# Attention on one core: one exponential less on ScalarE in every third unit, and a rounding copy on VectorE

## Chip, cores and metric

The kernel runs on one core of one Trainium2 chip (trn2). The metric is the device time of one execution in microseconds. Engines are named as in the profile: PE is TensorE's matmul, PEld its weight load, DVE is VectorE, ACT is ScalarE, POOL is GpSimd, SP is the engine that issues most DMAs.

## What is computed

A transformer block in fp32 on 48 x 48 tokens of 384 channels: layer norm, attention with 12 heads and a relative position bias, then a mixture-of-experts feed-forward. The change touches attention alone:

```python
attn = jnp.einsum('bqd,bkd->bqk', q * scale, k)
bias = (rel_h[..., :, None] + rel_w[..., None, :]).reshape(B * nh, S, S)
attn = jax.nn.softmax(attn + bias, axis=-1)
out = jnp.einsum('bqk,bkd->bqd', attn, v)
```

## The kernel before

TensorE multiplies in fp32r, a 4-byte type of less precision, so a value that needs full precision is kept as a pair: a high part, rounded to fp32r, and a low part, the value less its high part. Both go through TensorE.

A head has 2304 queries and 2304 keys. The queries are cut into 3 blocks of 768 columns (QBLOCKS = 3, QB = 768), the keys into 18 tiles of 128 rows (TILES = 18). One key tile against one query block is a **unit**: 54 units a head (UNITS), 648 in 12 heads. A unit goes through these steps:

- `scores`, TensorE, L851 to L865: four matmuls of 384 columns make the scores, 128 keys by 768 queries, in two of the four banks of ps_s. The bias and the subtraction of the row's maximum are in the operands (query_rest has the maximum in its last row).
- `exps`, ScalarE, L924 to L936: an exponential of the scores goes to p_hi, rounded to fp32r (L930), and a second exponential of the same scores goes to p_f in fp32 (L936). p_hi has a ring of 4 buffers, p_f has 2, so the second exponential of a unit waits until the low part two units back is made (L935).
- `low`, L718 to L723: p_lo = p_f - p_hi. VectorE makes it for two units of three and GpSimd (POOL) for the third, the one whose index leaves 2 when divided by POOL_EVERY = 3. `lo_done` (L712) gives the semaphore and the count for each.
- `pv`, TensorE, L867 to L875: four matmuls of the value tile with p_hi and p_lo add up the outputs and the softmax sums in ps_o, over the 18 units of a block.

The row maxima of the next head are made beside that. In each unit TensorE computes a chunk of 128 queries by 768 keys from the high parts alone, in two halves (`half`, L845), each into its own bank of ps_m, and VectorE reduces each half to a maximum (`reduce_half`, L971). A half is not started before the last one in its bank is reduced (L901, L910). When a query block is complete, a small maximum over the chunks gives neg_m (L969), which TensorE transposes, ScalarE copies, and SP takes to memory and back into query_rest.

The order is written out by hand for each engine, and each engine works through its own list in order. In step k of a head TensorE issues: the scores of unit k + 3 (LEAD), the first half of the chunk, pv of unit k, the second half (L877 to L911). VectorE issues: the maximum of the first half, the low part of unit k + 2 (LOW_LEAD) unless GpSimd has it, the maximum of the second half (L976 to L994). In the last unit of each block ScalarE and VectorE each copy half of ps_o to o_t (L945, L983). GpSimd's list (L827 to L841) is its low parts in order; behind two of the six of each block it also joins two partial outputs of a finished block: a copy of 32x384 (L821) and a sum of 32x384 (L823). In the last head the maxima end with step 11 (SHIFT = 12), since there is no next head: 606 units have maxima, 42 have none.

What the change touches: the semaphore at L687, which L930 signals and nothing waits for; `low` for GpSimd's units at L827 to L839; `exps` at L930; and VectorE's list at L989 to L991.

Of the kernel before, what the change touches and what calls it, by code (L numbers as in the profile page):

```python
# [12 lines left out]
ACT = mybir.ActivationFunctionType  # L13
# [11 lines left out]
TB = 384  # L25
# [353 lines left out]
UNITS = QBLOCKS * TILES  # L379
# [3 lines left out]
LOW_LEAD = 2  # L383
POOL_EVERY = 3
SHIFT = 12
RING = 4
# [257 lines left out]
def phase_attention(nc, q_hi_d, q_lo_d, k_hi_d, k_lo_d, rel_hi_d, rel_lo_d, v_d, m_d, o_d, sums_d, ident, keys, query_hi0, query_rest0, val0, mx, room):  # L644
# [11 lines left out]
    with ExitStack() as ctx:  # L656
        def sb(name, shape, dt=F32):
            return ctx.enter_context(nc.sbuf_tensor(name, shape, dt))

        def sem(name):  # L660
            return ctx.enter_context(nc.semaphore(name))
# [6 lines left out]
        p_hi = [sb(f"p_hi{i}", [P, 2, TB], F32R) for i in range(RING)]  # L668
        p_lo = [sb(f"p_lo{i}", [P, 2, TB], F32R) for i in range(RING)]
        p_both = sb("p_f", [P, 2, 2, TB])  # L670
        p_f = [p_both[:, i, :, :] for i in range(2)]
# [6 lines left out]
        ps_s = ctx.enter_context(nc.psum_tensor("ps_s", [P, 4, 512], F32))  # L678
# [5 lines left out]
        rest_in = [sem(f"rest_in{i}") for i in range(QBLOCKS)]  # L684
        m_out = sem("m_out")
        s_ok = sem("s_ok")
        hi_ok = sem("p_hi_ok")  # L687
        f_ok = sem("f_ok")
        lo_dve = sem("p_lo_dve")
        lo_pool = sem("p_lo_pool")  # L690
# [17 lines left out]
        def unit_at(par, k, lead=LEAD):  # L708

            return (par, k + lead) if k + lead < UNITS else (1 - par, k + lead - UNITS)  # L710

        def lo_done(h, idx):  # L712

            if idx % POOL_EVERY == POOL_EVERY - 1:
                return lo_pool, UNITS // POOL_EVERY * h + idx // POOL_EVERY + 1
            return lo_dve, (UNITS - UNITS // POOL_EVERY) * h + idx - idx // POOL_EVERY + 1

        def low(engine, n, par, idx):  # L718

            r = (2 * par + idx) % RING  # L720
            engine.wait_ge(f_ok, n + 3)
            engine.tensor_tensor(p_lo[r][:], p_f[idx % 2], p_hi[r][:].bitcast(F32),  # L722
                                 ALU.subtract).then_inc(lo_done(0, idx)[0], 1)  # L723
# [81 lines left out]
        @block.gpsimd  # L805
        def _(pool):
            for g in range(2):
                pool.sem_inc(ot_out[g], 32)
            def joined(h, par, b, c):

                g = (QBLOCKS * par + b) % 2

                pool.wait_ge(acc_a if c == 0 else acc_d, QBLOCKS * h + b + 2)
                at = TILES * (b + 1) + (1 + c) * POOL_EVERY - 1
                if at < UNITS:
                    pool.wait_ge(*lo_done(h, at))
                elif h < HEADS - 1:
                    pool.wait_ge(*lo_done(h + 1, at - UNITS))
                elif c == 0:
                    pool.wait_ge(*lo_done(h, UNITS - 1))  # L820
                pool.tensor_copy(o_low[g][:, c, :], o_t[g][HD:2 * HD, c, :]).then_inc(low_moved, 1)  # L821
                pool.wait_ge(low_moved, 2 * (QBLOCKS * h + b) + c + 1)
                pool.tensor_tensor(o_s[g][:, c, :], o_t[g][0:HD, c, :], o_low[g][:, c, :], ALU.add).then_inc(o_sum, 1)  # L823

            FIRST = 3 * POOL_EVERY

            def head(h, par, last=False):  # L827
                for idx in range(FIRST - 1, UNITS + FIRST - 1, POOL_EVERY):
                    if idx < UNITS:
                        low(pool, UNITS * h + idx, par, idx)  # L830
                    elif not last:
                        low(pool, UNITS * h + idx, 1 - par, idx - UNITS)
                    for b in range(QBLOCKS):
                        for c in range(2):
                            if idx == TILES * (b + 1) + (1 + c) * POOL_EVERY - 1:
                                joined(h, par, b, c)

            for idx in range(POOL_EVERY - 1, FIRST - 1, POOL_EVERY):
                low(pool, idx, 0, idx)  # L839
            for h in range(HEADS):  # L840
                head(h, h % 2, h == HEADS - 1)  # L841
# [80 lines left out]
        @block.scalar  # L922
        def _(act):
            def exps(h, par, idx, turn=None):  # L924
                n = UNITS * h + idx
                bank, r = 2 * (idx % 2), (2 * par + idx) % RING
                act.wait_ge(s_ok, n + 1)

                act.wait_ge(pv_ok, n + 1)
                act.activation(p_hi[r][:], ps_s[:, bank:bank + 2, 0:TB], ACT.Exp).then_inc(hi_ok, 1)  # L930
                if turn is not None:
                    act.copy(neg_mt[turn][:], ps_s[0:6, bank, TB:TB + P]).then_inc(negt_ok, 1)

                if UNITS * h + idx >= 2:
                    act.wait_ge(*(lo_done(h, idx - 2) if idx >= 2 else lo_done(h - 1, idx - 2 + UNITS)))  # L935
                act.activation(p_f[idx % 2], ps_s[:, bank:bank + 2, 0:TB], ACT.Exp).then_inc(f_ok, 1)  # L936

            def head(h, par, last=False):
                for k in range(UNITS):
                    if k % TILES == TILES - 1:  # L940
                        b = k // TILES
                        g = (QBLOCKS * par + b) % 2
                        act.wait_ge(pv_ok, UNITS * h + k + 1 + RING)
                        act.wait_ge(ot_out[g], out_count(h, par, b))
                        act.copy(o_t[g][:, 0, :], ps_o[0:VW, 0, 0:TB]).then_inc(acc_a, 1)  # L945
                    up, idx = unit_at(par, k)
                    if not (last and up != par):
                        exps(h + (up != par), up, idx, turned_at(k, last))

            def out_count(h, par, b):  # L950
                return 32 * ((QBLOCKS * par + b) // 2) + 32 * QBLOCKS * half(h, par) + 32

            def half(h, par):
                return (h - par) // 2

            act.sem_inc(acc_a, 1)
            act.sem_inc(f_ok, 2)
            for idx in range(LEAD):
                exps(0, 0, idx)
            for h in range(HEADS):  # L960
                head(h, h % 2, h == HEADS - 1)

        @block.vector
        def _(dve):
            def negated(count, s):

                if s % TILES == TILES - 1:
                    dve.wait_ge(mx_ok, 2 * count + 2)
                    dve.tensor_reduce(neg_m[s // TILES][:], mx[s // TILES][:], AX.X, ALU.max, negate=True).then_inc(neg_ok, 1)  # L969

            def reduce_half(count, s, c):  # L971
                dve.wait_ge(mm_ok, 2 * count + c + 1)
                col = s % 3 * 2 + c
                dve.tensor_reduce(mx[s // TILES][:, s // 3 % 6, col:col + 1], ps_m[:, c, 0:TB], AX.X, ALU.max).then_inc(mx_ok, 1)  # L974

            def head(h, par, last=False):  # L976
                for k in range(UNITS):
                    if k % TILES == TILES - 1:
                        b = k // TILES
                        g = (QBLOCKS * par + b) % 2  # L980
                        dve.wait_ge(pv_ok, UNITS * h + k + 1 + RING)
                        dve.wait_ge(ot_out[g], out_count(h, par, b))
                        dve.tensor_copy(o_t[g][:, 1, :], ps_o[0:VW, 1, 0:TB]).then_inc(acc_d, 1)  # L983
                    tp, s = chunk_at(h, par, k)
                    maxima = not (last and tp != par)
                    number = UNITS * (h + 1) + k - SHIFT
                    if maxima:
                        reduce_half(number, s, 0)
                    up, idx = unit_at(par, k, LOW_LEAD)  # L989
                    if not (last and up != par) and idx % POOL_EVERY < POOL_EVERY - 1:  # L990
                        low(dve, UNITS * h + k + LOW_LEAD, up, idx)  # L991
                    if maxima:
                        reduce_half(number, s, 1)
                        negated(number, s)  # L994

            def out_count(h, par, b):
                return 32 * ((QBLOCKS * par + b) // 2) + 32 * QBLOCKS * half(h, par) + 32

            def half(h, par):
                return (h - par) // 2  # L1000

            dve.sem_inc(acc_d, 1)
            dve.sem_inc(pv_ok, RING)
            dve.sem_inc(mm_ok, 2 * (UNITS - SHIFT))
            dve.sem_inc(mx_ok, 2 * (UNITS - SHIFT))
            dve.sem_inc(neg_ok, 2)
            for idx in range(LOW_LEAD):
                if idx % POOL_EVERY < POOL_EVERY - 1:
                    low(dve, idx, 0, idx)
            for h in range(HEADS):  # L1010
                head(h, h % 2, h == HEADS - 1)
# [889 lines left out]
```

## Time and profile before

| | us |
|---|---|
| median of 3 runs | 2230.9 |
| lowest and highest | 2229.8, 2233.19 |
| the profiled execution | 2227.99 |
| its span | 2226.2 |
| TensorE busy, share of the span | 94% |
| VectorE | 80% |
| ScalarE | 74% |
| GpSimd | 34% |

The span runs from the first to the last instruction in the trace; the time of the execution has a little around it. Attention lies between about 270 and 1418 us of the span. A duration in the views is that of the instruction from start to end; consecutive instructions of one engine overlap a little, so what one occupies is read from start to start.

### The profile page before, as it was taken

To read this page: it belongs to the slowest core of one execution; us is meant where nothing else is said; L and a number is where in the kernel's file an instruction comes from. 1 tells how busy PE (TensorE), PEld (TensorE's weight loads), DVE (VectorE), ACT (ScalarE), POOL (GpSimd) and SP (SyncE) were. 2 spreads that over 40 slices of the span, in tenths; PEclk is the share of its full clock that TensorE was granted. 3 is DMA by queue.
4 is the path that set the end of the run, shared out by engine and by line. 5 is a ranking of instruction groups with operands and counts; after the bars stand their busy time and mean duration, and the time that the engine had idled before them with its cause. 6 is when DMAs were issued, how large, how long until landed. Compare 5 with 4: busy or idle time off the path is not lost. (4 is left out here: it accounts for less than half of the span.)

```text
span 2226.2 us, 38086 instructions
## 1 busy us (share of the span) xinstructions
PE 2092.3 (94%) x12644; PEld 1936.4 (87%) x12644; DVE 1773.6 (80%) x3334; ACT 1650.6 (74%) x2908; POOL 755.4 (34%) x519
## 2 busy tenths in 40 slices
PE   6977899999999999999999999675999999999997
PEld 6977788888888888888888888463999999999997
DVE  5667899998999999999999996476777777777774
ACT  3354488888888888888888889412787777778785
POOL 0060045544444454454445545511121221111211
PEclk9955599999999999999999999786999999999999
DMA  6889876554655556365545632323666767666774
GB/s 212 240 246 301 249 136 107 106 102 74 133 88 109 90 106 117 74 117 102 107 83 101 131 75 70 98 106 108 198 219 216 222 220 221 216 217 215 215 219 108
DMA packets 121594, 338.20 MB, mean 152 GB/s; under 512 B 17984, under 2 KB 57496, under 8 KB 114740
## 3 DMA queue, kind: packets, MB, share of 16 engines
q1 hardware_dynamic: 109152, 308.88, 53.9%
q0 software_dynamic: 10400, 19.87, 4.1%
q10 hardware_dynamic: 1920, 7.88, 1.3%
q8 instruction: 69, 1.13, 0.2%
q14 instruction: 53, 0.43, 0.1%
HBM read 269.62 MB, written 66.97 MB: 151 GB/s over the span
## 5 line engine op out<-in xcount | busy, mean ns | idle before, releaser
L974 DVE TENSOR_REDUCE mx<-ps_m 128x1 f32<-128x384 f32 x1212 | 642.1, 552 | 100.8 <-PE ps_m L849 95.4
L722 POOL TENSOR_TENSOR p_lo<-p_f,p_hi 128x768 fp32r<-128x768 f32 x216 | 401.1, 1857 | 680.7 <-ACT p_f L936 680.7
L930 ACT ACTIVATE p_hi<-ps_s 128x768 fp32r<-128x768 f32 x648 | 528.4, 815 | 139.2 <-PE ps_s L863 135.9
L936 ACT ACTIVATE p_f<-ps_s 128x768 f32<-128x768 f32 x648 | 525.1, 810 | 1.3 <-POOL p_lo L722 1.3
L722 DVE TENSOR_TENSOR p_lo<-p_f,p_hi 128x768 fp32r<-128x768 f32 x432 | 418.9, 970 | 31.7 <-ACT p_f L936 30.8
L849 PE MATMUL ps_m<-all_keys,query_hi 128*128 128x384 f32 x1212 | 409.1, 342 | 7.6 <-DVE mx L974 7.6
L1644 ACT CAST w_hi<-w_raw 128x384 fp32r<-128x384 f32 x600 | 290.3, 516 | 134.2 <-PE ps_o L1621 128.3
L1762 DVE TENSOR_TENSOR w_lo<-w_raw,w_hi 128x384 fp32r<-128x384 f32 x600 | 316.5, 555 | 76.9 <-ACT w_hi L1644 76.7
L860 PE MATMUL ps_s<-query_hi,all_keys 128*128 128x384 f32 x1296 | 336.0, 340 | 5.0 <-SPq L783 4.1
L873 PE MATMUL ps_o<-p_hi,val 128*65 128x384 f32 x1296 | 330.8, 336 | 1.9 <-POOL p_lo L722 1.7
L863 PE MATMUL ps_s<-query_rest,all_keys 121*128 121x384 f32 x1296 | 331.8, 337 | 0.0
L873 PE MATMUL ps_o<-p_lo,val 128*65 128x384 f32 x1296 | 331.7, 337 | 0.0
L849 PEld LDWEIGHTS ps_m<-all_keys,query_hi 128*128 128x128 f32 x1212 | 226.9, 188 | 45.4 <-DVE mx L974 21.4
L1580 POOL DMA_INDIRECT out<-y,to_i x50 | 80.2, 1604 | 522.6 <-ACT y L1676 361.3
L860 PEld LDWEIGHTS ps_s<-query_hi,all_keys 128*128 128x128 f32 x1296 | 231.7, 188 | 15.2 <-SPq L782 4.5
L863 PEld LDWEIGHTS ps_s<-query_rest,all_keys 121*128 121x128 f32 x1296 | 236.9, 189 | 0.0
L873 PEld LDWEIGHTS ps_o<-p_lo,val 128*65 128x65 f32 x1296 | 175.3, 135 | 50.2
L1621 PE MATMUL ps_o<-w_hi,h_hi 128*128 128x384 f32 x600 | 206.7, 344 | 0.0
L1621 PE MATMUL ps_o<-w_hi,h_lo 128*128 128x384 f32 x600 | 202.8, 338 | 0.0
L1621 PE MATMUL ps_o<-w_lo,h_hi 128*128 128x384 f32 x600 | 202.6, 338 | 0.0
L873 PEld LDWEIGHTS ps_o<-p_hi,val 128*65 128x65 f32 x1296 | 176.0, 136 | 29.4 <-POOL p_lo L722 4.2
L1798 DVE TENSOR_TENSOR h_lo<-h_f,h_hi 128x256 fp32r<-128x256 f32 x300 | 127.6, 425 | 42.8 <-ACT h_f L1670 37.5
(199 smaller groups left out, 2999.0 us busy)
## 6 DMA issues: line engine op xcount, KB each, us to landing
w_raw<-w_u SPq DMA_DIRECT2D x200, 576.0 KB, 4.8
query_rest<-rel_lo_d SPq DMA_DIRECT2D x36, 864.0 KB
query_rest<-q_hi_d SPq DMA_DIRECT2D x36, 576.0 KB
query_rest<-q_lo_d SPq DMA_DIRECT2D x36, 576.0 KB
rel_hi_d<-room SPq DMA_DIRECT2D x6, 2016.0 KB, 13.7
rel_lo_d<-out_lo SPq DMA_DIRECT2D x6, 2016.0 KB, 18.6
query_hi<-rel_hi_d SPq DMA_DIRECT2D x24, 432.0 KB, 18.8
v_d<-v_sb SPq DMA_DIRECT2D x6, 1170.0 KB, 8.0
```

The costliest lines, as they stand in the source:

```text
L722: engine.tensor_tensor(p_lo[r][:], p_f[idx % 2], p_hi[r][:].bitcast(F32), ALU.subtract).then_inc(lo_done(0, idx)[0], 1)
L849: pe.matmul(ps[:, c, 0:TB], query_hi[tp][:, tile], key_hi[tp][:, keys], start=True, stop=True).then_inc(mm_ok, 1)
L860: pe.matmul(ps_s[:, bank + c, 0:TB], key_hi[par][:, j * P:(j + 1) * P], query_hi[par][:, b * QB + c * TB:b * QB + (c + 1) * TB], start=Tru ...
L863: last = pe.matmul(ps_s[:, bank + c, 0:TB], key_rest[par][:, j * P:(j + 1) * P], query_rest[b][0:TOP, j // 3, c * TB:(c + 1) * TB], start= ...
L873: last = pe.matmul(ps_o[0:VW, c, 0:TB], val[par][:, j, :], part[r][:, c, :], start=(j == 0 and part is p_hi), stop=(j == TILES - 1 and par ...
L930: act.activation(p_hi[r][:], ps_s[:, bank:bank + 2, 0:TB], ACT.Exp).then_inc(hi_ok, 1)
L936: act.activation(p_f[idx % 2], ps_s[:, bank:bank + 2, 0:TB], ACT.Exp).then_inc(f_ok, 1)
L974: dve.tensor_reduce(mx[s // TILES][:, s // 3 % 6, col:col + 1], ps_m[:, c, 0:TB], AX.X, ALU.max).then_inc(mx_ok, 1)
L1621: mm = pe.matmul(ps_o[:, t, 0:C], v[w][:, f, cut], wt[w][:, f, :], start=(q + f + m == 0), stop=(q == QUARTERS - 1 and f == FC - 1 and m = ...
L1644: act.copy(hi[par][:, j % KC, :], raw[par][:, j % KC, :]).then_inc(whi_ok, 1)
L1762: low = dve.tensor_tensor(lo[par][:, k, :], raw[par][:, k, :], hi[par][:, k, :].bitcast(F32), ALU.subtract)
L1798: dve.tensor_tensor(h_lo[w][:, f, :], h_f[:, f, :], h_hi[w][:, f, :].bitcast(F32), ALU.subtract).then_inc(g_lo, 1)
```

## The change

In GpSimd's units ScalarE leaves out the exponential into p_hi. VectorE fills p_hi by a copy of p_f that rounds to fp32r, at the place in its list where it makes the low part of other units. GpSimd waits for that copy (semaphore cast_ok) before its low part. The old semaphore p_hi_ok goes. 648 exponentials into p_hi become 432; 216 copies of 128x768 are new; all else stands as it was.

```diff
--- before.py
+++ after.py
@@ -684,7 +684,7 @@
         rest_in = [sem(f"rest_in{i}") for i in range(QBLOCKS)]
         m_out = sem("m_out")
         s_ok = sem("s_ok")
-        hi_ok = sem("p_hi_ok")
+        cast_ok = sem("cast_ok")
         f_ok = sem("f_ok")
         lo_dve = sem("p_lo_dve")
         lo_pool = sem("p_lo_pool")
@@ -715,6 +715,9 @@
                 return lo_pool, UNITS // POOL_EVERY * h + idx // POOL_EVERY + 1
             return lo_dve, (UNITS - UNITS // POOL_EVERY) * h + idx - idx // POOL_EVERY + 1
 
+        def rounded_by_dve(idx):
+            return idx % POOL_EVERY == POOL_EVERY - 1
+
         def low(engine, n, par, idx):
 
             r = (2 * par + idx) % RING
@@ -826,6 +829,8 @@
 
             def head(h, par, last=False):
                 for idx in range(FIRST - 1, UNITS + FIRST - 1, POOL_EVERY):
+                    if idx < UNITS or not last:
+                        pool.wait_ge(cast_ok, (UNITS * h + idx) // POOL_EVERY + 1)
                     if idx < UNITS:
                         low(pool, UNITS * h + idx, par, idx)
                     elif not last:
@@ -836,6 +841,7 @@
                                 joined(h, par, b, c)
 
             for idx in range(POOL_EVERY - 1, FIRST - 1, POOL_EVERY):
+                pool.wait_ge(cast_ok, idx // POOL_EVERY + 1)
                 low(pool, idx, 0, idx)
             for h in range(HEADS):
                 head(h, h % 2, h == HEADS - 1)
@@ -927,7 +933,8 @@
                 act.wait_ge(s_ok, n + 1)
 
                 act.wait_ge(pv_ok, n + 1)
-                act.activation(p_hi[r][:], ps_s[:, bank:bank + 2, 0:TB], ACT.Exp).then_inc(hi_ok, 1)
+                if not rounded_by_dve(idx):
+                    act.activation(p_hi[r][:], ps_s[:, bank:bank + 2, 0:TB], ACT.Exp)
                 if turn is not None:
                     act.copy(neg_mt[turn][:], ps_s[0:6, bank, TB:TB + P]).then_inc(negt_ok, 1)
 
@@ -987,7 +994,10 @@
                     if maxima:
                         reduce_half(number, s, 0)
                     up, idx = unit_at(par, k, LOW_LEAD)
-                    if not (last and up != par) and idx % POOL_EVERY < POOL_EVERY - 1:
+                    if not (last and up != par) and rounded_by_dve(idx):
+                        dve.wait_ge(f_ok, UNITS * h + k + LOW_LEAD + 3)
+                        dve.tensor_copy(p_hi[(2 * up + idx) % RING][:], p_f[idx % 2]).then_inc(cast_ok, 1)
+                    elif not (last and up != par):
                         low(dve, UNITS * h + k + LOW_LEAD, up, idx)
                     if maxima:
                         reduce_half(number, s, 1)
```

## Rows read from the trace of the kernel before

**Rows 1.** Busy time by stretch: us, busy (count) per engine, PEclk, DMA share, GB/s.
```profile
700.00:800.00 100.00, 99.42 (x566) 89.19 (x565) 90.30 (x157) 86.61 (x119) 48.08 (x31) 1.00 0.56 102
```

**Rows 2.** Costliest groups, whole span: busy us, mean ns, idle before and its releaser.
```profile
L974 DVE TENSOR_REDUCE mx<-ps_m 128x1 f32<-128x384 f32 x1212 | 642.1, 552 | 100.8 <-PE ps_m L849 95.4
...
L930 ACT ACTIVATE p_hi<-ps_s 128x768 fp32r<-128x768 f32 x648 | 528.4, 815 | 139.2 <-PE ps_s L863 135.9
```

**Rows 3.** VectorE in time, one cycle: start us, us, what, [idle before <-releaser].
```profile
827.88 1.01 DVE L974 TENSOR_REDUCE mx<-ps_m 128x1 f32<-128x384 f32 x2
829.11 0.56 DVE L974 TENSOR_REDUCE mx<-ps_m 128x1 f32<-128x384 f32 x1 [0.23 <-PE ps_m L849]
829.99 0.56 DVE L974 TENSOR_REDUCE mx<-ps_m 128x1 f32<-128x384 f32 x1 [0.32 <-PE ps_m L849]
830.46 0.95 DVE L722 TENSOR_TENSOR p_lo<-p_f,p_hi 128x768 fp32r<-128x768 f32 x1
831.33 1.02 DVE L974 TENSOR_REDUCE mx<-ps_m 128x1 f32<-128x384 f32 x2
832.26 0.95 DVE L722 TENSOR_TENSOR p_lo<-p_f,p_hi 128x768 fp32r<-128x768 f32 x1
833.13 1.01 DVE L974 TENSOR_REDUCE mx<-ps_m 128x1 f32<-128x384 f32 x2
```

**Rows 4.** GpSimd in time, the same cycle.
```profile
827.91 1.85 POOL L722 TENSOR_TENSOR p_lo<-p_f,p_hi 128x768 fp32r<-128x768 f32 x1 [0.88 <-ACT p_f L936]
833.13 1.85 POOL L722 TENSOR_TENSOR p_lo<-p_f,p_hi 128x768 fp32r<-128x768 f32 x1 [3.38 <-ACT p_f L936]
```

**Rows 5.** All engines in time, 1338.9 to 1341.3 us.
```profile
1338.92 1.01 POOL L823 TENSOR_TENSOR o_s<-o_t,o_low 32x384 f32<-32x384 f32 x1
...
1338.94 1.81 DVE L722 TENSOR_TENSOR p_lo<-p_f,p_hi 128x768 fp32r<-128x768 f32 x1
...
1340.67 1.01 DVE L974 TENSOR_REDUCE mx<-ps_m 128x1 f32<-128x384 f32 x2
...
1341.27 0.19 PEld L849 LDWEIGHTS ps_m<-all_keys,query_hi 128*128 128x128 f32 x1 [0.78 <-DVE mx L974]
```

**Rows 6.** GpSimd and VectorE in time, where the maxima have ended.
```profile
1357.63 1.84 POOL L722 TENSOR_TENSOR p_lo<-p_f,p_hi 128x768 fp32r<-128x768 f32 x1 [2.96 <-ACT p_f L936]
...
1358.97 1.32 DVE L722 TENSOR_TENSOR p_lo<-p_f,p_hi 128x768 fp32r<-128x768 f32 x1 [2.07 <-ACT p_f L936]
...
1364.76 1.04 POOL L821 COPY o_low<-o_t 32x384 f32<-32x384 f32 x1
```

**Rows 7.** A wider maximum (groups), and one-input operations on SBUF (VectorE in time).
```profile
L598 DVE TENSOR_REDUCE mx<-ps_c 128x2 f32<-128x768 f32 x42 | 39.4, 949 | 14.2 <-PE ps_c L528 13.8
...
1524.01 0.29 DVE L1708 TENSOR_SCALAR sel<-rank 128x144 fp32r<-128x144 f32 x1 [2.52 <-POOL every L1556]
...
1524.44 0.23 DVE L1710 TENSOR_SCALAR first<-rank 128x144 f32<-128x144 f32 x1
...
1531.04 0.17 DVE L1739 TENSOR_SCALAR row_i<-at_i 128x36 int32<-128x36 int32 x1
```

**Rows 8.** TensorE in time, the same cycle.
```profile
830.48 0.34 PE L849 MATMUL ps_m<-all_keys,query_hi 128*128 128x384 f32 x1
...
831.52 0.51 PE L873 MATMUL ps_o<-p_hi,val 128*65 128x384 f32 x2
...
832.22 0.34 PE L849 MATMUL ps_m<-all_keys,query_hi 128*128 128x384 f32 x1
```

**Rows 9.** VectorE: first and last maximum, a neg_m maximum, and the copy's group.
```profile
271.99 0.56 DVE L974 TENSOR_REDUCE mx<-ps_m 128x1 f32<-128x384 f32 x1 [0.25 <-PE ps_m L849]
...
1352.80 0.55 DVE L974 TENSOR_REDUCE mx<-ps_m 128x1 f32<-128x384 f32 x1
...
1353.39 0.19 DVE L969 TENSOR_REDUCE neg_m<-mx 128x6 f32<-128x36 f32 x1
...
L983 DVE COPY o_t<-ps_o 65x384 f32<-65x384 f32 x36 | 19.6, 545 | 3.7 <-PE ps_o L873 3.7
```

## The prediction, made before the changed kernel was seen

> **What bounds the kernel now.** I read the stretch view first. In 700 to 800 us, the middle of attention, TensorE is busy 99.42 of 100 us at the full granted clock, VectorE 90.30, ScalarE 86.61, GpSimd 48.08 [rows 1]. So TensorE sets the pace and VectorE stands close behind it; an exponential taken from ScalarE lightens an engine that is third. The groups give the counts: 1212 half-block maxima, two for each of 606 units, and 648 exponentials of 0.815 us into p_hi [rows 2].
>
> Then one cycle of three units in order of time. I call A a unit whose low part GpSimd makes, and A+1 and A+2 the two behind it, whose low parts VectorE makes. VectorE's list [rows 3]: two maxima back to back take 1.01 us against 0.55 for one, so one occupies it for 0.46; from the start of such a pair to the next instruction it is 0.93 (831.33 to 832.26); a low part occupies 0.87 (830.46 to 831.33). The only idle time is 0.23 + 0.32 = 0.55 us, ahead of two maxima and ended by TensorE. The cycle lasts 5.22 to 5.25 us (827.88 to 833.13); GpSimd's low parts start 5.22 us apart [rows 4], and I take 5.23. GpSimd's low part of A takes 1.85 us, 827.91 to 829.76; VectorE's low part of A+1 starts 0.70 us later, at 830.46. The two never overlap, and that is an accident of when each gets its input.
>
> What happens if they do overlap is in two other places. At 1338.92 GpSimd starts a 1.01 us sum; VectorE's low part, sent 0.02 us later, lasts 1.81 us in place of 0.95, and the next maximum starts at 1340.67, 0.74 us after GpSimd's end at 1339.93. TensorE then waits 0.78 us for that maximum [rows 5]. And at 1358.97 a low part comes in the middle of GpSimd's of 1357.63 to 1359.47 and ends at 1360.29, 0.82 us after GpSimd's end [rows 6]. So a low part on VectorE does not run beside GpSimd's: it waits for nearly all of the rest of it, and TensorE has no store of work to cover that.
>
> **The change, part by part.**
>
> Removed: 216 exponentials of 0.815 us on ScalarE [rows 2]. Worth nothing in time: ScalarE's own idle time, 139.2 us, ends by TensorE's scores in 135.9 of it [rows 2], and TensorE is busy beside it. The input p_f of A is there up to 0.8 us earlier, but the new reader is VectorE, whose list is in order, and the cast stands behind the first maximum of step A-2. The 216 skipped signals of the old semaphore had no reader.
>
> Added on VectorE: 216 casts of 128x768 from p_f to p_hi, SBUF to SBUF. The trace has none. Upper end: one element at a time, as the low part: 0.95 long, 0.87 occupied [rows 3]; a 128x768 maximum says the same, 0.949 [rows 7]. Lower end: the one-input operations on SBUF. With 36 columns one takes 0.17, with 144 columns 0.23 [rows 7], so 108 more cost about 0.06, or 0.55 ns a column; the maxima pay 949 - 552 = 397 ns for 384 more, or 1.03 [rows 2, 7]. At 0.55 a cast of 768 is 0.17 + 732 x 0.55 ns = 0.57. I take 0.55 long and 0.46 occupied, as a 384-column maximum. Against it speaks the one such row that writes the cast's type, fp32r: 0.29 for 144 columns; but it also reads its input reordered, so I give the slow cast a lesser chance. By the Trainium skill, VectorE: DVE Perf Modes, the perf-mode tier table, an fp32 tensor_copy between SBUF tensors goes two elements a cycle; worked out from its 1227 ns for 2048 elements and 0.96 GHz that is an estimate of 0.56 us here, and the sum would stay as below.
>
> Moved: GpSimd's low part of A starts after the cast instead of after the exponential. In the cycle shown, the first maximum of step A-2 starts at 827.88 + 0.46 = 828.34, the cast at 828.80, so GpSimd starts at 828.80 + 0.55 + 0.08 (its start behind the exponential, as now within 0.1 us) = 829.43 and ends at 831.28, not 829.76. That covers the moment at which VectorE wants its low part of A+1, 830.46. This is the step that costs. Behind the blocked low part on VectorE's queue stand the maxima, which TensorE waits for, since its two banks of ps_m are refilled only when read.
>
> The new cycle, counted from the start of the cast, VectorE's list: cast 0 to 0.46; two maxima, 0.46 to 1.39; low part of A+1 asks at 1.39. GpSimd runs from 0.55 + 0.08 = 0.63 to 2.48. The low part then lets the next start 0.74 after that [rows 5], 3.22. Two maxima to 4.15; low part of A+2 to 5.02; two maxima to 5.95; next cast. Is VectorE ever idle in it? TensorE issues its half of step A once the maximum at 3.22 is done (3.77); its weights come in 0.05 later and take 0.19 [rows 5], the matmul 0.34 [rows 8], so it ends by 4.35, before VectorE wants it at 5.02. From there TensorE makes a half each 0.87 us (830.48 to the next but one at 832.22 [rows 8]): 5.22, 6.09, 6.96, against wants at 5.48, 6.41 and 6.88. So it is idle for 0.1 us at most, and that in front of the blocked low part, where it costs nothing. ScalarE: p_f of A+2 needs GpSimd's end, 2.48, and is ready an exponential later, at 3.35, wanted at 4.15. GpSimd's result is wanted by TensorE at about 2.5; TensorE has some 0.7 us of wait in a cycle to cover it. So the cycle is 5.95 in place of 5.23. 606 / 3 = 202 cycles x 0.72 = **145 us**.
>
> What lay in VectorE's idle time now adds. 33 copies of ps_o (0.545 long [rows 9], 0.47 occupied): 15.5. 34 small maxima for neg_m (0.19 long [rows 9], with the wait around it 0.22 more): 7.5. In 66 cycles GpSimd goes on from its low part to joining two sums. Its copy is blocked in turn by VectorE's low part of A+1 (such a copy took 1.04 us [rows 6]); I put the end of the copy 0.4 after 3.30, its sum from 3.77 to 4.78 (1.01 [rows 5]), and that blocks the low part of A+2, sent at 4.15: next start at 4.78 + 0.74 = 5.52, not 5.02. 66 x 0.50 = 33. Its bounds are 0 (the sum is over by 4.15) and the whole sum, 0.9, so 0 to 60 us.
>
> Together: 202 x 5.95 + 15.5 + 7.5 + 33 = 1258 us for the stretch with maxima. Now it lasts from 271.99 to 1353.35 [rows 9], 1081.4 us. **+176.5 us.** The 25 us by which it now exceeds 202 x 5.23 are block edges and blocks like that at 1338.94; they fall into TensorE's new waits and are not counted twice. The last 42 units have no maxima. There VectorE has room, ScalarE loses 14 exponentials and p_f waits on a later GpSimd: between -14 x 0.8 = -11 and 14 x 1.1 = +15 us (a cast and GpSimd's later end in full). I take 0.
>
> The profiled execution took 2227.99 us with a span of 2226.2; 2228.0 + 176.5 = 2404.5. It stands 2.9 under the median of 2230.9, so **2407**.
>
> **The rivals.**
>
> Slow cast (chance 0.17). If fp32r output keeps the cast at one element at a time: GpSimd 1.03 to 2.88, next start 3.62, cycle 3.62 + 0.93 + 0.87 + 0.93 = 6.35, which is 0.40 x 202 = 81 more: 2488. For it: the 0.29 row; against it: the 0.17 and 0.23 rows.
>
> No block, TensorE keeps the pace (0.07): the end on the other side, not slower. Its place is the low part of A+1. If it could run beside GpSimd's, VectorE would need 6 x 0.465 + 2 x 0.87 + 0.46 = 4.99 us of 5.23, and the rest fits narrowly: GpSimd ends at 831.28, TensorE wants the part at 831.52 [rows 8]; p_f of A+2 then ends at about 832.15, wanted at 832.26. It decides from the point at which the blocked 0.82 us shrink under the 0.24 that is left. Time: 2231, from -5 to +10 us. Against it: [rows 5, 6], the same two operations on the same tiles. A gain beyond noise would need ScalarE to be the bound; it may be in the last 42 units, at most 11 us. That is the faster side, 0.03: 2224.
>
> Half a block (0.08). If GpSimd's part starts earlier than I say, or the low part slides ahead of it in some cycles, the cycle falls to about 5.6: 2231 + 202 x 0.37 + 30 = 2336.
>
> **How the numbers follow.** The forecast has 0.65. Its own range comes from the joined sums (-33, +27), the tail (-11, +15) and 0.04 us on the cycle (8): 2370 to 2450. To hold 8 in 10 I stretch it over the slow cast and leave out the half block and the unblocked cases: 2370 to 2495. A measurement of this kernel tells about 0.2%, 4.5 us, from no change. Faster 0.03; same 0.05 (most of no block); slower 0.92.
>
> **What would show it.** VectorE over 98% busy in 700 to 800 us, TensorE about 88 to 90%, ScalarE nearer 66%, 17 cycles of three units in 100 us in place of 19. The low parts of A+1 would last 1.8 to 1.95 us, each ending 0.82 after GpSimd's end, the others 0.95; the cast would be 0.55 long. ps_m on TensorE would wait for the maximum once a cycle, some 0.5 to 0.8 us. The forecast is wrong if all low parts stay at 0.95, if the cast is 0.95 long, or if the granted clock in attention falls under 1.00 with TensorE's new gaps; no row has attention with such gaps at length, and I leave that outside.

## The result, and the profile after

The changed kernel takes 2408.8 us (median of 4 runs, 2407.4 to 2414.9) against 2232.1 for the kernel before in the same comparison: ratio 1.0794, 95% interval 1.0777 to 1.0811. The forecast was 2407. The profiled execution has a span of 2405.6 us, 179.4 more than before.

Busy time by stretch, the view of [rows 1], of the changed kernel:

```profile
700.00:800.00 100.00, 91.55 (x485) 73.49 (x483) 99.35 (x152) 65.26 (x88) 39.71 (x26) 1.00 0.52 96
```

VectorE rose from 90.30 to 99.35 of 100 us, TensorE fell from 99.42 to 91.55, ScalarE is down to 65.26, and the granted clock stayed at 1.00 with TensorE's new gaps. The costliest groups and the cast's (busy us, mean ns, idle before and who ended it):

```profile
L725 POOL TENSOR_TENSOR p_lo<-p_f,p_hi 128x768 fp32r<-128x768 f32 x216 | 398.1, 1843 | 872.4 <-DVE p_hi L999 590.3
L943 ACT ACTIVATE p_f<-ps_s 128x768 f32<-128x768 f32 x648 | 524.9, 810 | 204.6 <-POOL p_lo L725 183.7
L725 DVE TENSOR_TENSOR p_lo<-p_f,p_hi 128x768 fp32r<-128x768 f32 x432 | 625.2, 1447 | 17.0 <-ACT p_f L943 16.3
L981 DVE TENSOR_REDUCE mx<-ps_m 128x1 f32<-128x384 f32 x1212 | 633.3, 546 | 7.2 <-PE ps_m L855 0.5
...
L999 DVE CAST p_hi<-p_f 128x768 fp32r<-128x768 f32 x216 | 121.2, 561 | 0.2
```

The maxima cost as much as in [rows 2], but VectorE's idle time before them, 100.8 us, is down to 7.2. The casts add 121 us. The largest item is neither: it is the 432 low parts. Their work did not change, and they grew from 0.970 us each to 1.447, 206 us in all. Their group in the kernel before:

```profile
L722 DVE TENSOR_TENSOR p_lo<-p_f,p_hi 128x768 fp32r<-128x768 f32 x432 | 418.9, 970 | 31.7 <-ACT p_f L936 30.8
```

One cycle in time shows which of them, and why (VectorE and GpSimd, the answer to [rows 3, 4]):

```profile
1449.10 0.55 DVE L999 CAST p_hi<-p_f 128x768 fp32r<-128x768 f32 x1
1449.56 1.12 DVE L981 TENSOR_REDUCE mx<-ps_m 128x1 f32<-128x384 f32 x2
...
1449.72 1.85 POOL L725 TENSOR_TENSOR p_lo<-p_f,p_hi 128x768 fp32r<-128x768 f32 x1 [4.09 <-ACT p_f L943]
...
1450.60 1.78 DVE L725 TENSOR_TENSOR p_lo<-p_f,p_hi 128x768 fp32r<-128x768 f32 x1
...
1452.30 1.01 DVE L981 TENSOR_REDUCE mx<-ps_m 128x1 f32<-128x384 f32 x2
1453.24 0.94 DVE L725 TENSOR_TENSOR p_lo<-p_f,p_hi 128x768 fp32r<-128x768 f32 x1
```

GpSimd runs from 1449.72 to 1451.57. VectorE's low part of A+1, sent at 1450.60, lasts 1.78 us and ends 0.81 after GpSimd's end; that of A+2 lasts 0.94. In the stretch with maxima 201 low parts of VectorE lie over one of GpSimd's in this way: they last 1.76 to 1.90 us, each ends 0.81 to 0.82 after GpSimd's end, and the next instruction starts 0.73 to 0.75 after it. (The view names p_f as what GpSimd waited for at 1449.72. The cast that ended at 1449.65 has read that same p_f, so the cast was the later of the two; the group above puts 590 of GpSimd's 872 us of idle time down to the cast.) From cast to cast such a cycle is 5.94 us (1443.16 to 1449.10). TensorE waits at two places of it, in order of time:

```profile
1446.96 0.19 PEld L855 LDWEIGHTS ps_m<-all_keys,query_hi 128*128 128x128 f32 x1 [0.73 <-DVE mx L981]
...
1448.76 0.19 PEld L855 LDWEIGHTS ps_m<-all_keys,query_hi 128*128 128x128 f32 x1 [0.16 <-DVE mx L981]
```

### The profile page after: what moved, and what is told of

It is laid out like the page before. It is cut to its first block and busy times, and to the rows that moved or that the text cites. A ratio compares the mean times of both kernels' runs of the same rounds, so it can differ in the third digit from the quotient of the medians.

```text
span 2405.6 us, 38302 instructions
## 1 busy us (share of the span) xinstructions
PE 2172.7 (90%) x12644; PEld 1904.6 (79%) x12644; DVE 2060.3 (86%) x3550; ACT 1524.2 (63%) x2692; POOL 744.5 (31%) x519
## 5 line engine op out<-in xcount | busy, mean ns | idle before, releaser
L943 ACT ACTIVATE p_f<-ps_s 128x768 f32<-128x768 f32 x648 | 524.9, 810 | 204.6 <-POOL p_lo L725 183.7
L725 DVE TENSOR_TENSOR p_lo<-p_f,p_hi 128x768 fp32r<-128x768 f32 x432 | 625.2, 1447 | 17.0 <-ACT p_f L943 16.3
L981 DVE TENSOR_REDUCE mx<-ps_m 128x1 f32<-128x384 f32 x1212 | 633.3, 546 | 7.2 <-PE ps_m L855 0.5
L855 PE MATMUL ps_m<-all_keys,query_hi 128*128 128x384 f32 x1212 | 438.5, 366 | 83.9 <-DVE mx L981 83.8
L937 ACT ACTIVATE p_hi<-ps_s 128x768 fp32r<-128x768 f32 x432 | 351.5, 814 | 244.5 <-PE ps_s L869 244.5
L879 PE MATMUL ps_o<-p_hi,val 128*65 128x384 f32 x1296 | 336.1, 340 | 26.3 <-POOL p_lo L725 26.2
L879 PEld LDWEIGHTS ps_o<-p_hi,val 128*65 128x65 f32 x1296 | 160.2, 136 | 79.4 <-POOL p_lo L725 47.4
```

Source lines behind the costliest of these rows:

```text
L855: pe.matmul(ps[:, c, 0:TB], query_hi[tp][:, tile], key_hi[tp][:, keys], start=True, stop=True).then_inc(mm_ok, 1)
L879: last = pe.matmul(ps_o[0:VW, c, 0:TB], val[par][:, j, :], part[r][:, c, :], start=(j == 0 and part is p_hi), stop=(j == TILES - 1 and par ...
```

## The experiments

The theory is the forecast's **block**: a low part on VectorE doesn't run beside GpSimd's work on the same kind of operands, and the cast pushed GpSimd's low part over the moment at which VectorE's comes. Against it stand **volume** (the cast's own time on a nearly full VectorE) and **lateness** (GpSimd's result comes 1.5 us later, and p_f's two buffers and TensorE wait for that).

Where only the order of VectorE's list changes, the diff is that of the list in words.

**The cast two maxima earlier**

```diff
 in step k of VectorE's list
   reduce_half(number, s, 0)
-  cast of unit k + 2, or low part of unit k + 2
+  low part of unit k + 2, unless it is GpSimd's
+  cast of unit k + 3, if it is GpSimd's
   reduce_half(number, s, 1)
```

> The changed kernel with the cast moved forward on VectorE's list by two maxima, to right behind the low part of unit A-1. Same instructions, same counts. Block theory (VectorE's low part of A+1 waits for GpSimd's of A): counted from the cast, VectorE asks for that low part at 0.46 + 4 x 0.46 = 2.3 us in place of 1.39, GpSimd still ends at 2.48, so nearly nothing is left of the block; VectorE's list then takes 5.0 us a cycle. The maximum behind the cast comes 0.46 later, which TensorE feels: 0.5 + 0.87 + 0.5 + 0.87 + 0.93 + 0.87 + 0.46 + 0.55 = 5.55 us round that loop, so cycles of 5.25 to 5.55 and 2250 to 2320 us. Volume theory (the cast's own time on VectorE is what costs, wherever it stands): no change, 2409.

Measured: 2302.3 us, ratio 1.0325 (1.0301 to 1.0348). Two low parts and what lies between, VectorE in time:

```profile
888.34 0.95 DVE L725 TENSOR_TENSOR p_lo<-p_f,p_hi 128x768 fp32r<-128x768 f32 x1
889.20 0.55 DVE L985 CAST p_hi<-p_f 128x768 fp32r<-128x768 f32 x1
889.67 1.65 DVE L981 TENSOR_REDUCE mx<-ps_m 128x1 f32<-128x384 f32 x3
891.64 0.56 DVE L981 TENSOR_REDUCE mx<-ps_m 128x1 f32<-128x384 f32 x1 [0.32 <-PE ps_m L855]
892.11 1.00 DVE L725 TENSOR_TENSOR p_lo<-p_f,p_hi 128x768 fp32r<-128x768 f32 x1
```

The same instructions in another order give back 106 of the 177 us. The block is gone (0.95 to 1.00 us), VectorE waits for TensorE again, and what closes the cycle is the loop: a maximum frees its bank, TensorE refills the bank, and the maximum behind that needs the new scores. Without a join such a cycle is 5.56 us, against 5.55 expected; the one shown has a join, 5.63 (this cast to the next, at 894.83). Volume falls.

**The cast one maximum earlier**

```diff
 in step k of VectorE's list
+  cast of unit k + 2, if it is GpSimd's
   reduce_half(number, s, 0)
-  cast of unit k + 2, or low part of unit k + 2
+  low part of unit k + 2, unless it is GpSimd's
```

> The changed kernel with the cast moved forward by one maximum, ahead of the first maximum of its step. Block theory: VectorE asks at 1.85 us after the start of the cast, GpSimd ends at 2.48 as before, the rest is unchanged: 5.48 us a cycle in place of 5.95, 202 x 0.47 = 95 us less, 2314. Volume theory: no change, 2409. Theory that GpSimd's late result holds TensorE directly: 0.46 earlier on GpSimd too, so it would also fall, but the low part of A+1 would keep its length.

Measured: 2314.3 us, ratio 1.0375 (1.0354 to 1.0397), as the block has it to the microsecond. The cycle is 5.47 us (GpSimd's low parts start at 700.07 and 705.54), and the low part of A+1 is shorter by the 0.5 that it now comes later:

```profile
704.92 0.54 DVE L985 CAST p_hi<-p_f 128x768 fp32r<-128x768 f32 x1
705.38 1.64 DVE L981 TENSOR_REDUCE mx<-ps_m 128x1 f32<-128x384 f32 x3
706.94 1.26 DVE L725 TENSOR_TENSOR p_lo<-p_f,p_hi 128x768 fp32r<-128x768 f32 x1
```

**GpSimd only writes**

```diff
             engine.wait_ge(f_ok, n + 3)
+            if idx % POOL_EVERY == POOL_EVERY - 1:
+                engine.memset(spare[:], 0.0)
+                engine.memset(p_lo[r][:].bitcast(F32), 0.0).then_inc(lo_pool, 1)
+                return
             engine.tensor_tensor(p_lo[r][:], p_f[idx % 2], p_hi[r][:].bitcast(F32),
                                  ALU.subtract).then_inc(lo_done(0, idx)[0], 1)
```

Two more lines make room for `spare`: it is allocated, and o_low has one buffer in place of two.

> The changed kernel, but GpSimd's low part becomes two fills with zero (128x1152 of a spare tile, then p_lo), which wait for the same cast and take about the same time (1.06 + 0.7 us) and read nothing; the low parts of these units are left out of the result. Block theory, with a block only where both engines read SBUF: low parts on VectorE fall back to 0.95 us, cycles to 5.23, 2232 to 2260 us. Lateness theory (GpSimd's part comes 1.5 us later than before, and p_f and TensorE wait for that): GpSimd's end does not move, so it stays at 2400 to 2410.

Measured: 2278.8 us, ratio 1.0209 (1.0191 to 1.0228). GpSimd is as late as in the changed kernel and about as long, and 130 of the 177 us are gone, so lateness explains at most the rest. It came out above the range. One reason is in the trace: a low part beside the fills is free, one beside the joining sum, which still reads, is not (VectorE and GpSimd in time):

```profile
884.32 1.06 POOL L727 MEMSET spare<- 128x1152 f32 x1 [2.28 <-DVE p_hi L1004]
...
885.23 0.95 DVE L730 TENSOR_TENSOR p_lo<-p_f,p_hi 128x768 fp32r<-128x768 f32 x1
...
885.31 0.74 POOL L728 MEMSET p_lo<- 128x768 f32 x1
...
886.76 1.00 POOL L831 TENSOR_TENSOR o_s<-o_t,o_low 32x384 f32<-32x384 f32 x1
...
887.02 1.56 DVE L730 TENSOR_TENSOR p_lo<-p_f,p_hi 128x768 fp32r<-128x768 f32 x1
```

The stretch with maxima takes 1130.4 us there, 49 more than in the kernel before. By kinds of cycle, each the mean of its kind: with a join 5.73 us (883.71 to 889.44) in place of 5.16, 66 x 0.58 = 38; with VectorE's copy of ps_o 6.50 in place of 5.79, 33 x 0.71 = 23; plain ones 5.09 (to 894.53) in place of 5.27, 12 less; with neg_m no change. The second term is lateness. The last unit of a block is an A, so the copy stands behind GpSimd's late part: at 638.63 TensorE waits 0.34 us for it, and at 639.59 VectorE's copy 0.24 for TensorE. So lateness does cost here, up to 23 us. In the changed kernel TensorE waits at the same place too, 0.65 us at 677.55, but VectorE is then still in its blocked low part, and its copy at 678.71 comes without a wait.

The Trainium skill, SBUF — State Buffer, section Who interferes with whom, states this as a rule: a VectorE instruction with two SBUF inputs contends with a GpSimd instruction that reads SBUF, and not with one that only writes it. The two rows 885.23 and 887.02 agree on both halves of it.

**Three buffers of p_f**

```diff
-        p_both = sb("p_f", [P, 2, 2, TB])
+        p_both = sb("p_f", [P, 3, 2, TB])
...
-                    act.wait_ge(*lo_done(h, idx - 2))
+                    act.wait_ge(*lo_done(h, idx - 3))
```

> The changed kernel with three buffers of p_f in place of two, so that ScalarE waits for the low part three units back (o_low has one buffer in place of two, to make room). ScalarE now waits 184 us in all for GpSimd's low parts. Block theory: those waits are not on the path, the low part of A+1 is blocked as before: 2409, within 5. Lateness theory by way of p_f: up to 180 us faster.

Measured: 2408.5 us, ratio 1.0795 (1.0777 to 1.0813). ScalarE's wait for GpSimd fell from 183.7 us to 2.7, and the time did not move:

```profile
L943 ACT ACTIVATE p_f<-ps_s 128x768 f32<-128x768 f32 x648 | 522.6, 808 | 43.2 <-PE ps_s L869 40.3 <-POOL p_lo L725 2.7
```

The idle time moved to ScalarE's waits for TensorE's scores, ahead of p_hi from 244.5 us to 382.3. ScalarE's wait for GpSimd was off the path. Lateness by way of p_f falls.

**A late GpSimd without a cast** (two runs on the kernel before; the second waits for `+ 2`)

```diff
             engine.wait_ge(f_ok, n + 3)
+            if idx % POOL_EVERY == POOL_EVERY - 1 and n - LOW_LEAD < UNITS * (HEADS - 1) + SHIFT:
+                engine.wait_ge(mx_ok, 2 * (n - LOW_LEAD + UNITS - SHIFT) + 1)
```

> The kernel before, both exponentials on ScalarE and no cast. GpSimd's low part of A waits, besides, for the end of the first maximum of step A-2, where the changed kernel's cast would start. Block theory: GpSimd runs from 0.63 to 2.48 us after that maximum's start, VectorE asks for the low part of A+1 at 1.39, gets on at 3.22, and the list closes at 5.48: 202 x 0.25 = 50 us for the cycles and up to 30 for block edges and joins, 2280 to 2313 us. Volume theory: VectorE has no more work, so 2232.

Measured: 2327.3 us, ratio 1.0423 (1.0386 to 1.0460).

> The same with the second maximum of step A-2: GpSimd starts another 0.46 us later, at about 1.09 after the start of the first, and ends at 2.93. Block theory: the low part of A+1, asked for at 1.39, lets the next start at 3.67, the list closes at 5.93: nearly the changed kernel's time without a cast, 2375 to 2404 us. Volume theory: 2232.

Measured: 2449.2 us, ratio 1.0971 (1.0934 to 1.1009). Nothing was added to any engine's work, and the time rose by more than the change makes it: the cast's own time is not needed for the loss. GpSimd is late in these two as well as in VectorE's way; what lateness alone costs is bounded by the run in which it only writes. Both came out above their ranges. In the second, VectorE in time:

```profile
879.59 2.05 DVE L724 TENSOR_TENSOR p_lo<-p_f,p_hi 128x768 fp32r<-128x768 f32 x1
...
885.31 0.56 DVE L976 TENSOR_REDUCE mx<-ps_m 128x1 f32<-128x384 f32 x1 [0.31 <-PE ps_m L851]
885.79 2.00 DVE L724 TENSOR_TENSOR p_lo<-p_f,p_hi 128x768 fp32r<-128x768 f32 x1
```

I had closed the cycle by VectorE's list alone. But after the block TensorE is behind, and without the cast VectorE comes 0.31 us too soon to the maximum before the low part of A+1: the cycle is the loop through TensorE, 6.20 us here (879.59 to 885.79), 6.16 in most plain ones, against 5.93; in the first of the two it is 5.53 (GpSimd's starts, 881.00 and 886.53) against 5.48, with 0.32 us of the same idle time. Over 202 cycles that is 46 us and 10 us, of the 45 and 14 by which they lie above their ranges. In the changed kernel, whose plain cycle is 5.94, the cast stands in that gap. So its own 0.46 us are, by this comparison, partly free: they fill time that the block opened.

**One maximum made twice, on the kernel before**

```diff
+                    if maxima and unit_at(par, k, LOW_LEAD)[1] % POOL_EVERY == POOL_EVERY - 1:
+                        dve.wait_ge(mm_ok, 2 * number + 1)
+                        dve.tensor_reduce(again[:], ps_m[:, 0, 0:TB], AX.X, ALU.max)
                     if maxima:
                         reduce_half(number, s, 0)
```

> The kernel before with one maximum in three units made twice (a 128x384 maximum from PSUM, 0.46 us occupied, as long as the cast, and no reader of SBUF), at the cast's place. Block theory: VectorE then has 4.99 us of work in 5.23, GpSimd starts as before: 2232 to 2250 us. Volume theory: at least 202 x 0.46 = 93 us more, 2325.

Measured: 2235.4 us, ratio 1.0015 (0.9998 to 1.0032). VectorE is busy 96.96 of 100 us and TensorE 99.02. It is as much work as the cast, one maximum ahead of the cast's place, and costs 0.3% at most, where the changed kernel loses 7.9%.

**The low part of A+1 behind the second maximum, the cast in its place**

```diff
 in step k of VectorE's list
-  low part of unit k + 2
+  low part of unit k + 2, if it is an A+2
   reduce_half(number, s, 1)
+  low part of unit k + 2, if it is an A+1
```

> The changed kernel with the cast where it is, and VectorE's low part of A+1 put behind the second maximum of its step instead of ahead of it. Block theory: it is asked for at 1.85 us after the cast's start in place of 1.39, GpSimd ends at 2.48 as before, so 0.46 us of the wait is filled with a maximum: 5.49 us a cycle, 2316 us, from 2300 to 2340. Volume theory: no change, 2409.

Measured: 2308.5 us, ratio 1.0304 (1.0289 to 1.0318), on a chip where the kernel before took 2239.4 in place of 2232. The cycle is 5.50 us (GpSimd's starts, 699.75 and 705.25), so volume falls again, and so does lateness: GpSimd's low part starts 0.63 us after the cast's start (704.62), as in the changed kernel, and 100 us are gone. The number is the expected one, but not by the expected way (GpSimd and VectorE in time):

```profile
705.25 1.84 POOL L725 TENSOR_TENSOR p_lo<-p_f,p_hi 128x768 fp32r<-128x768 f32 x1 [3.67 <-DVE p_hi L999]
...
706.52 0.56 DVE L981 TENSOR_REDUCE mx<-ps_m 128x1 f32<-128x384 f32 x1 [0.32 <-PE ps_m L855]
707.00 0.95 DVE L725 TENSOR_TENSOR p_lo<-p_f,p_hi 128x768 fp32r<-128x768 f32 x1
```

The third maximum waits 0.32 us for TensorE, so the low part of A+1 is sent 0.09 us before GpSimd's end at 707.09 and keeps its 0.95: the block is gone, not shortened. The loop through TensorE closes this cycle. That it does so within 0.02 us of where the rest of the block would have is chance.

**GpSimd rounds for itself**

```diff
+            def rounded(h, par, idx, n):
+                pool.wait_ge(f_ok, n + 3)
+                pool.tensor_copy(p_hi[(2 * par + idx) % RING][:], p_f[idx % 2]).then_inc(cast_ok, 1)
+                pool.wait_ge(cast_ok, n // POOL_EVERY + 1)
...
```

GpSimd does this where it waited for VectorE's cast, which is gone.

> The changed kernel, but GpSimd makes the rounding copy itself, as soon as p_f of A is there, 0.7 us earlier than in the kernel before; VectorE has the work of the kernel before. By the rows of before GpSimd's copy, sent while VectorE makes the low part of A-1, gets on when that ends (827.96) and takes about 0.9 us, its low part runs to about 830.8, and the low part of A+1, asked for at 830.46, is blocked for 0.3 us. Block theory: 2235 to 2290 us. If the copy takes twice as long, the block grows by 0.9 us: up to 2420. Volume theory: 2232 whatever GpSimd does.

Measured: 2276.6 us, ratio 1.0167 (1.0153 to 1.0182). The kernel before took 2239.4 in this comparison too. GpSimd's copy took 0.81 us where nothing was in its way and 1.22 to 1.55 behind a low part of VectorE's. The number lies in the range, but the block of 0.3 us in each cycle did not come: plain cycles are 5.26 us, against 5.27 in the kernel before, and those with neg_m 5.25 against 5.48. The loss is in the cycles with a join, 5.78 against 5.16, 66 x 0.63 = 41 us. It is the cheapest way found to take the exponential off ScalarE, and still a loss; whether it stays one when the join is moved has not been tried.

**The joining sum behind the low part of A+2** (changed kernel) **and of A+1** (kernel before)

```diff
                 pool.wait_ge(low_moved, 2 * (QBLOCKS * h + b) + c + 1)
+                if at + 2 < UNITS:
+                    pool.wait_ge(*lo_done(h, at + 2))
+                elif h < HEADS - 1:
+                    pool.wait_ge(*lo_done(h + 1, at + 2 - UNITS))
```

The version of the kernel before has `at + 1` in place of `at + 2`.

> The changed kernel with GpSimd's joining sum (66 cycles with maxima) held back until VectorE's low part of A+2 is made. Block theory: that low part is no longer blocked by the sum (0.46 us in each of these cycles), but the next cast meets the sum's end for some 0.2 us: 66 x 0.26 = 17 us less, 2392, from 2379 to 2400. If the joins don't block: 2409.

Measured: 2391.0 us, ratio 1.0679 (1.0663 to 1.0694): 17.8 us under the changed kernel's 2408.8, which is of another comparison; in this one the kernel before took 2239.4. What the expectation charged for the cast is there: in 65 cycles it lasts 0.7 us in place of 0.55, over the end of GpSimd's sum (GpSimd and VectorE in time), so the cast with its one input waits for GpSimd too.

```profile
314.52 1.01 POOL L830 TENSOR_TENSOR o_s<-o_t,o_low 32x384 f32<-32x384 f32 x1 [1.59 <-DVE p_lo L725]
...
315.23 0.73 DVE L1003 CAST p_hi<-p_f 128x768 fp32r<-128x768 f32 x1
```

> The kernel before with GpSimd's joining sum held back until VectorE's low part of A+1 is made, so that it can no longer block that part as it does at 1338.94 us. About ten low parts of 432 last over 1.1 us in the kernel before; each costs up to 0.74 us: 5 us less at best, 2227 to 2232.

Measured: 2229.5 us, ratio 0.9954 (0.9942 to 0.9966), more than the blocks in the trace can give: 17 low parts last over 1.1 us in the kernel before, and only three of them (1.81 us each) stand in the stretch with maxima.

> The same kernel as the one before it, measured again, since the kernel before itself ran at 2239 us in that comparison and at 2232 us in the others, and its own profile explains only some 5 us. If the sum that may or may not get in ahead of VectorE's low part makes the difference, this one stays at 2227 to 2231 and the ratio is under 1 by 0.1 to 0.5%. If the gain belonged to that occasion, the ratio is 1.000 within 0.001.

Measured: 2229.3 us, ratio 0.9996 (0.9987 to 1.0006). The gain did not come again, on another chip. This version took the same 2229 us both times; it was the kernel before that took 2239.4 on the one chip and 2230.6 on the other. Whether that belongs to the chip or to the occasion stays open. No version is shown to beat the kernel before.

## Why the prediction was right

**The cycle.** Forecast 5.95 us, measured 5.94. Its parts: cast 0.46 to the next start; the two maxima behind it 1.04 where I had 0.93, which is the idle 0.1 us that I put there; GpSimd's start 0.07 after the cast's end; the next start 0.73 after GpSimd's end (0.74). The low part of A+1 lasts 1.78, at the edge of the 1.8 to 1.95 given, because it is sent that 0.1 later.

**The sum.** The stretch with maxima runs from 270.31 to 1529.48 us, 1259.2, against 1258. Part by part: 202 x 5.94 = 1199.9. A cycle with VectorE's copy of ps_o is 6.60 us, 0.66 more and not 0.47: the copy occupies 0.47, and the maximum behind it comes another 0.2 us later, for which I had no term (in the kernel before 0.15, at the same place): 33 x 0.66 = 21.8. With neg_m 6.15, 0.21 more: 7.1. With a join 6.40, 0.46 more and not 0.50: 66 x 0.46 = 30.4. Together 1259.2. One term was 6 us too small, another 3 too large, and the cycles 2 too large; that they cancel to 1 us is luck. In time, a copy of ps_o:

```profile
678.71 0.54 DVE L990 COPY o_t<-ps_o 65x384 f32<-65x384 f32 x1
679.38 0.56 DVE L981 TENSOR_REDUCE mx<-ps_m 128x1 f32<-128x384 f32 x1
```

The join's copy and sum behaved as I put them:

```profile
840.41 1.04 POOL L824 COPY o_low<-o_t 32x384 f32<-32x384 f32 x1
841.52 1.00 POOL L826 TENSOR_TENSOR o_s<-o_t,o_low 32x384 f32<-32x384 f32 x1
...
841.94 1.41 DVE L725 TENSOR_TENSOR p_lo<-p_f,p_hi 128x768 fp32r<-128x768 f32 x1
```

The tail without maxima, from there to the end of the last join (1597.43; before, 1353.35 to 1418.35), took 68.0 us in place of 65.0: 3 us, taken as 0. The start of attention came 1.7 us earlier. 177.8 + 3.0 - 1.7 = 179.1 of the 179.4 by which the span grew.

**The removed exponentials** were put at nothing, and the sum closes without a term for them: ScalarE's load fell by 21 points. No run takes them away and changes nothing else. Nearest is the one in which GpSimd rounds for itself: plain cycles stay at 5.26 us, and the 33 with neg_m are 0.23 shorter, which I have not taken apart.

**The cast** is 0.561 us, the fast end, as a 384-column maximum. The one row that spoke for the slow cast, the fp32r output at 0.29, did not decide; its reordered input is then the likelier cause, which no run here separates. The 0.561 agrees with the estimate of 0.56 worked out from the Trainium skill, VectorE: DVE Perf Modes, the perf-mode tier table.

**The rivals.** No block: the run in which GpSimd only writes is that world, as far as the low parts go, and it is 130 us faster. It stands at 2279 and not at the rival's 2231, since the joining sum still blocks and GpSimd is late at the block ends. Half a block is what one maximum of distance gives, 2314 where I had put such a world at 2336.

**Off:** TensorE's busy share, 91.55 where I said 88 to 90; TensorE waits for a maximum twice a cycle, 0.73 and 0.16 us, where I said once; and the reasoning that VectorE's list alone closes the cycle. It does in the changed kernel, by 0.1 us of idle time, and does not as soon as the cast is taken away.

## What to carry to other kernels

Before a wait is put in front of GpSimd's work, write out in time which two-input instructions and casts of VectorE it will then fall beside, and add the overlap once per cycle. A copy that an almost full VectorE has room for may cost little itself and much by where it moves GpSimd; its place on the list is worth as much as its length. And a long wait on an engine in the profile (184 us on ScalarE) does not tell by itself that it costs time: here it was taken away and the time stayed.

## What the runs showed that I had not expected

A block can cost more than VectorE's list shows: with nothing to fill the time in which TensorE catches up, 6.16 us a cycle in place of 5.93. An expectation can also be met by another way than the one it states, as in two of the runs above (2308.5 and 2276.6 us), so the lengths of the instructions have to be looked at beside the time. And the kernel before had a median of 2239 us in one comparison of five, in place of 2231 to 2232, so a ratio within 0.5% of 1 needs a second comparison on another chip.
